# Two attention stages: one-bank units of maxima, a fourth score bank, three weighings in L1, the last folds on VectorE

## The reference

```python
# L0: 8 heads of 16; L1: 16 heads of 32 (with layer norms before its projections)
scores = einsum('bqhd,bkhd->bhqk', Qh, Kh) * scale
attn = softmax(scores, axis=-1)
ctx = einsum('bhqk,bkhd->bqhd', attn, Vh)
# then W_o, residual, and a feed-forward block
```

## Time and profile before

| | us |
|---|---|
| median of three runs | 6442.13 (6438.35 to 6446.0) |
| the profiled execution | 6450.87 |
| its span, first to last instruction | 6449.1 |
| PE busy / PE weight loads busy | 5748.3 / 3457.8 |
| DVE / ACT / POOL busy | 3664.2 / 3201.7 / 2617.4 |

### The profile page before, as it was taken

How to read it: one execution, slowest core, us unless ns; L and a number is a source line. 1 busy time by engine, 2 the same in 40 slices (tenths; PEclk the granted TensorE clock), 3 DMA queues, 4 the chain that set the end, 5 groups by cost and what they waited for, 6 DMA issues and landing times. The chain is left out here.

```text
span 6449.1 us, 99761 instructions
## 1 busy us (share of the span) xinstructions
PE 5748.3 (89%) x29508; PEld 3457.8 (54%) x29508; DVE 3664.2 (57%) x4012; ACT 3201.7 (50%) x5857; POOL 2617.4 (41%) x1284
## 2 busy tenths in 40 slices
PE   5869999999666569999999999999999997659999
PEld 4734444444255445555555555555555553447777
DVE  4457777777433556666666666666666663521111
ACT  3327776777422335555555555555555564022222
POOL 0000000000000028888888888888888886000000
PEclk9969999999878779999999999999999998779999
DMA  3431111111342321111111111111011102820000
GB/s 106 124 87 34 35 33 34 33 33 29 93 153 86 93 75 35 29 36 35 38 36 35 27 37 36 36 38 36 25 37 37 36 24 74 258 72 26 26 26 14
DMA packets 335740, 347.84 MB, mean 54 GB/s; under 512 B 183664, under 2 KB 187632, under 8 KB 333296
## 3 DMA queue, kind: packets, MB, share of 16 engines
q1 hardware_dynamic: 335344, 342.99, 19.9%
HBM read 227.57 MB, written 115.21 MB: 53 GB/s over the span
## 5 line engine op out<-in xcount | busy, mean ns | idle before, releaser
L750 DVE TENSOR_REDUCE a_maxes<-a_mscore 128x1 f32<-128x802 f32 (+1 forms) x3072 | 2931.6, 988 | 1360.5 <-PE a_mscore L787 1344.8
L732 ACT ACTIVATE a_prob<-a_score 128x512 f32<-128x512 f32 x4992 | 2600.4, 605 | 1524.2 <-PE a_score L797 1517.5
L797 PE MATMUL a_score<-a_q,a_k 97*128 97x512 f32 (+1 forms) x4992 | 1956.2, 446 | 64.4 <-ACT a_prob L732 39.7
L704 POOL TENSOR_TENSOR a_added<-a_added,a_prob 128x1024 f32<-128x1024 f32 x768 | 1829.1, 2382 | 230.9 <-ACT a_prob L732 181.9
L787 PE MATMUL a_mscore<-a_k,a_qm 96*128 96x512 f32 (+5 forms) x6144 | 1734.7, 400 | 85.2 <-DMA a_k<-k 55.7
L787 PEld LDWEIGHTS a_mscore<-a_k,a_qm 96*128 96x128 f32 (+1 forms) x6144 | 1483.5, 311 | 317.1 <-DVE a_maxes L750 226.0
L816 PE MATMUL a_acc<-a_prob,a_v 128*32 128x512 f32 x9984 | 1611.9, 608 | 0.0
L797 PEld LDWEIGHTS a_score<-a_q,a_k 97*128 97x128 f32 (+1 forms) x4992 | 885.7, 191 | 1311.6 <-ACT a_prob L732 800.3
L701 POOL TENSOR_TENSOR a_added<-a_prob 128x1024 f32<-128x1024 f32 x128 | 303.5, 2371 | 2562.7 <-ACT a_prob L732 2562.6
L811 PE MATMUL a_acc<-a_prob,a_ones 128*1 128x512 f32 x2048 | 966.2, 594 | 0.0
L1121 DVE TENSOR_TENSOR f_hl<-f_h,f_hh 128x512 fp32r<-128x512 f32 x160 | 110.7, 692 | 672.5 <-ACT f_hh L1100 672.5
(11 more groups left out here) (143 smaller groups left out, 3728.4 us busy)
## 6 DMA issues: line engine op xcount, KB each, us to landing
a_qm<-q SPq DMA_DIRECT2D x384, 64.0 KB, 1.8
a_q<-q SPq DMA_DIRECT2D x384, 64.0 KB, 1.8
acc<-a_acc_sb SPq DMA_DIRECT2D x384, 64.0 KB
o_part<-acc SPq DMA_DIRECT2D x24, 1024.0 KB, 11.0
a_k<-k SPq DMA_DIRECT2D x48, 416.0 KB, 5.8
mid<-o_xout SPq DMA_DIRECT2D x16, 1024.0 KB, 8.3
f_X<-mid SPq DMA_DIRECT2D x16, 1024.0 KB, 6.3
q<-pq_out SPq DMA_DIRECT2D x128, 128.0 KB, 2.1
```

The costliest lines, as they stand in the source:

```text
L704: pool.tensor_tensor(added[:], added[:], prob[:, 3 * i + 1:3 * i + 3], ALU.add).then_inc(add_done, 1)
L732: act.activation(prob[:, t], score[SCORES[it.j][t]][:], ACT.Exp, scale=SCALE).then_inc(exp_done, 1)
L750: dve.tensor_reduce(maxes[j][:, t, c:c + 1], mscore[u % 2][:, lo:hi], AX.X, ALU.max).then_inc(unit_read, 1)
L797: pe.matmul(score[SCORES[it.j][t]][:], kt[it.k][r:r + C, i * P:(i + 1) * P], qt[it.j][r:r + C, :], start=True, stop=True).then_inc(score_d ...
```

## The change

- Four score banks in place of three; they go round and round (`score_bank`), and a score waits for the exp of four tiles before.
- Three tiles of maxima of one bank in place of two of two. A unit is one matmul and one reduction: in L0 32 units an item (416 or 386 columns, the half of the array changes with each, opposite to that of the score tile beside it where there is one unit), in L1 28 (458 columns). A unit waits for the reduction that last used its bank, in most cases that of three units before.
- Each score tile has a unit beside it. In L0 tiles 3, 11 and 19 have three, in L1 tiles 3 and 18 have two. `early` is 16 in L0, 10 in L1.
- L1 is weighed in three batches of three slots, after tiles 9 (the item before's last), 15 and 25. `copy_at` moves from step 4 to 5.
- POOL makes seven additions an item (`ADDS`). The last three, of 512 columns each, go to DVE (`fold`), after its unit of tile 6 in the next item. POOL's first addition of an item waits for the first fold of the item before.

```diff
@@ -421,13 +421,12 @@
 GROUPS = ST // 2
-SCORES = [([0, 1, 2] * ST)[:ST], ([0, 2, 1] * ST)[:ST]]
-CHUNKS = 4
-UNITS = (NB // P) * CHUNKS
+BANKS = 4
 QB = T // NB
 class Layout:
@@ -448,39 +447,49 @@
             self.at = {0: (5, True), 2: (6, True), 4: (0, False), 6: (1, False), 8: (2, False), 10: (3, False),
                        12: (4, False)}
             self.copy_at = 3
-            self.units_at = (0, 2, 3, 5, 6, 8, 10, 11, 13, 15, 16, 18, 19, 21, 23, 24)
-            self.early = 8
+            self.CHUNKS, extra, self.early = 8, {3: 2, 11: 2, 19: 2}, 16
         else:
             self.ROWS, self.SIDE, self.SUMS = 128, 3, 1
             self.slots = [[(0, 3 * i), (1, 3 * i + 1), (2, 3 * i + 2), (3, ("one", 3 * i))] for i in range(8)]
             self.slots.append([(0, 24), (1, 25), (3, ("sum", None))])
-            self.batches = [[0, 1], [2, 3], [4, 5], [6, 7], [8]]
-            self.at = {1: (3, True), 3: (4, True), 5: (0, False), 8: (1, False), 11: (2, False)}
-            self.copy_at = 4
-            self.units_at = (0, 2, 3, 4, 6, 7, 8, 10, 11, 12, 15, 17, 18, 21, 23, 24)
-            self.early = 6
+            self.batches = [[0, 1, 2], [3, 4, 5], [6, 7, 8]]
+            self.at = {4: (2, True), 7: (0, False), 12: (1, False)}
+            self.copy_at = 5
+            self.CHUNKS, extra, self.early = 7, {3: 1, 18: 1}, 10
         self.HALVES = P // self.ROWS
         self.COLS = SPAD // self.HALVES
         self.NBATCH = len(self.batches)
+        self.UNITS = NB // P * self.CHUNKS
         tiles = [[t for i in b for _, t in self.slots[i] if not isinstance(t, tuple)] for b in self.batches]
         self.opens = {min(ts): b for b, ts in enumerate(tiles)}
         self.closes = [max(ts) for ts in tiles]
+        self.units_at, made = [], 0
+        for t in range(ST):
+            more = 1 + extra.get(t, 0)
+            self.units_at.append(range(made, made + more))
+            made += more
+        assert made == self.UNITS
+        bank = [i % 3 for i in range(2 * self.UNITS)]
+        if bank[-1] == 0:
+            bank[-1] = 1
+        self.bank = [bank[:self.UNITS], bank[self.UNITS:]]
+        around = bank + bank
+        self.back = [[next(d for d in range(1, 6) if around[at - d] == around[at])
+                      for at in range(i, i + self.UNITS)] for i in (2 * self.UNITS, self.UNITS)]
     def key_tile(self, t):
         return t % self.HALVES, t // self.HALVES
     def chunk(self, c):
-        if self.HALVES == 1:
-            wide = -(-S // (2 * CHUNKS)) * 2
-            lo, hi = c * wide, min((c + 1) * wide, S)
-            return [(0, at, min(NB, hi - at), at - lo) for at in range(lo, hi, NB)]
-        a = self.COLS // CHUNKS
-        rest = S - self.COLS
-        b = -(-rest // (2 * CHUNKS)) * 2
-        return [(0, c * a, a, NB - a), (1, c * b, min(b, rest - c * b), NB)]
+        half, at = (1 - c % 2, c // 2) if self.HALVES == 2 else (0, c)
+        keys = min(self.COLS, S - half * self.COLS)
+        wide = -(-keys // (2 * (self.CHUNKS // self.HALVES))) * 2
+        return half, at * wide, min(wide, keys - at * wide)
 class Item:
@@ -505,7 +514,8 @@
-ADDS = 10
+ADDS, FOLDS, FOLD_AT = 7, 3, 6
 def attention(nc, name, H, hd, q, k, v, row, acc_out, sums_out):
@@ -523,7 +533,7 @@
     APART = SUMS == 1
     PAIRS = H // 2
     LAST_KEYS = S - (ST - 1) * P
-    EARLY = L.early
+    UNITS, CHUNKS = L.UNITS, L.CHUNKS
     ACC_ROWS = P if not APART else 3 * 32 + 1
     with phase(nc, name) as (ctx, sb, ps, sem):
@@ -540,8 +550,8 @@
             ones = sb("ones", [P, 1], F32)
             added, total = sb("added", [P, 2, NB], F32), sb("total", [P, NB], F32)
-        score = [ps(f"score{i}", [P, NB]) for i in range(3)]
-        mscore = [ps(f"mscore{i}", [P, 2 * NB]) for i in range(2)]
+        score = [ps(f"score{i}", [P, NB]) for i in range(BANKS)]
+        mscore = [ps(f"mscore{i}", [P, NB]) for i in range(3)]
         acc = ps("acc", [P, NB])
         k_loaded = [sem(f"k_loaded{i}") for i in range(2)]
@@ -553,7 +563,7 @@
         filled = sem("filled")
         score_done, exp_done, pv_done = sem("score_done"), sem("exp_done"), sem("pv_done")
         unit_done, unit_read, neg_done = sem("unit_done"), sem("unit_read"), sem("neg_done")
-        add_done, acc_copied = sem("add_done"), sem("acc_copied")
+        add_done, fold_done, acc_copied = sem("add_done"), sem("fold_done"), sem("acc_copied")
         acc_stored = [sem(f"acc_stored{i}") for i in range(2)]
         LOADS = 16 * 3 * HALVES
@@ -577,24 +587,13 @@
                 yield from pair(p, False, False)
             yield from pair(PAIRS - 1, False, True)
-        def score_free(it, t):
-            b = SCORES[it.j][t]
-            same = [u for u in range(t) if SCORES[it.j][u] == b]
-            if same:
-                return it.n * ST + same[-1] + 1
-            if it.first:
-                return None
-            return it.n * ST + max(u for u in range(ST) if SCORES[1 - it.j][u] == b) + 1 - ST
-        def units_of(it, half_step):
-            if half_step not in L.units_at:
-                return None
-            u = L.units_at.index(half_step) + EARLY
-            if u < UNITS:
-                return None if it.last else (1, u)
-            return None if it.last_two else (2, u - UNITS)
+        def score_bank(it, t):
+            return (t + ST % BANKS * it.j) % BANKS
+        def units_of(it, t):
+            found = [divmod(u + L.early, UNITS) for u in L.units_at[t]]
+            return [(1 + more, u) for more, u in found if not (it.last or (it.last_two and more))]
@@ -692,27 +691,17 @@
             for it in items(pool) if APART else ():
-                base = it.n * ADDS
-                for i in range(1, 8):
+                for i in range(1, ADDS + 1):
                     pool.wait_ge(exp_done, it.n * ST + 3 * i + 3)
                     if i == 1:
                         if not it.first:
-                            pool.wait_ge(add_done, base)
+                            pool.wait_ge(fold_done, it.n * FOLDS - FOLDS + 1)
                         pool.tensor_tensor(added[:], prob[:, 1:3], prob[:, 4:6], ALU.add).then_inc(add_done, 1)
                     else:
-                        pool.wait_ge(add_done, base + i - 1)
+                        pool.wait_ge(add_done, it.n * ADDS + i - 1)
                         pool.tensor_tensor(added[:], added[:], prob[:, 3 * i + 1:3 * i + 3],
                                            ALU.add).then_inc(add_done, 1)
-                pool.wait_ge(exp_done, it.n * ST + ST)
-                pool.wait_ge(add_done, base + 7)
-                pool.tensor_tensor(added[:, 0], added[:, 0], prob[:, 24], ALU.add).then_inc(add_done, 1)
-                pool.tensor_tensor(added[0:LAST_KEYS, 1], added[0:LAST_KEYS, 1], prob[0:LAST_KEYS, 25],
-                                   ALU.add).then_inc(add_done, 1)
-                pool.wait_ge(add_done, base + 9)
-                if not it.first:
-                    pool.wait_ge(pv_done, it.n * NBATCH)
-                pool.tensor_tensor(total[:], added[:, 0], added[:, 1], ALU.add).then_inc(add_done, 1)
         @block.scalar
         def _(act):
@@ -728,8 +717,10 @@
                     b = L.opens[t]
                     act.wait_ge(pv_done, it.n * NBATCH - NBATCH + b + 1)
                     if APART:
-                        act.wait_ge(add_done, it.n * ADDS - ADDS + 2 * b + 1)
-                act.activation(prob[:, t], score[SCORES[it.j][t]][:], ACT.Exp, scale=SCALE).then_inc(exp_done, 1)
+                        act.wait_ge(add_done, it.n * ADDS - ADDS + min(L.batches[b][-1], ADDS))
+                        if b == NBATCH - 1:
+                            act.wait_ge(fold_done, it.n * FOLDS)
+                act.activation(prob[:, t], score[score_bank(it, t)][:], ACT.Exp, scale=SCALE).then_inc(exp_done, 1)
             for it in items(act):
                 for s in range(GROUPS):
@@ -744,15 +735,29 @@
         def _(dve):
             def maximum(n, j, use, u):
                 t, c = divmod(u, CHUNKS)
-                pieces = L.chunk(c)
-                lo, hi = pieces[0][3], pieces[-1][3] + pieces[-1][2]
+                _, _, wide = L.chunk(c)
                 dve.wait_ge(unit_done, n * UNITS + u + 1)
-                dve.tensor_reduce(maxes[j][:, t, c:c + 1], mscore[u % 2][:, lo:hi], AX.X, ALU.max).then_inc(unit_read, 1)
+                dve.tensor_reduce(maxes[j][:, t, c:c + 1], mscore[L.bank[j][u]][:, 0:wide], AX.X,
+                                  ALU.max).then_inc(unit_read, 1)
                 if u == UNITS - 1:
                     dve.wait_ge(unit_read, n * UNITS + UNITS)
                     if not (isinstance(n, int) and n < 2):
                         dve.wait_ge(row_stored[j], use * 16)
                     dve.tensor_reduce(negmax[j][:], maxes[j][:], AX.X, ALU.max, negate=True).then_inc(neg_done, 1)
+            def fold(n):
+                dve.wait_ge(add_done, n * ADDS + ADDS)
```

(67 more changed lines are left out.)

## The result

The changed kernel takes 7150.11 us (median of 4 runs, 7144.84 to 7160.17), the kernel before beside it 6440.24 (4 runs, 6438.31 to 6446.0): a ratio of 1.110, 95% interval 1.108 to 1.112. That is inside the range (6390 to 7170) and on the side that was given the most chance, but it is not the case that was forecast (6460). It is the rival "held twice by POOL" (7046, given 0.27), with clock falls on top. The profiled execution took 7160.17, span 7158.4.

The account below looks back on a forecast made before the run. No engine full; PE, issuing in order, waits for DVE's reductions. Profiled 6450.87 +112 (a0) -102 (a1) +6 (folds) +2 (starts) = 6469, less 9 to the runs' median: 6460 us; own range 6400 to 6550, 8 in 10 6390 to 7170.

Parts of the forecast that it names:

- Four score banks: Both attentions: the fourth bank buys nothing; in a0 the scores' wait for exps goes and a wait for DVE replaces it.
- held twice by POOL: Rival, a1: POOL's additions hold the second and third fold, third slot 4.6 us late, +586, 7046 us; chance 0.27.
- clock falls: PE's clock drops while it stands: up to 3.6 us an item, 461 in a1, up to 115 in a0's odd items.
- the forecast case: Whole kernel: the walks of both attentions plus the folds, 6460 us, own range 6400 to 6550, chance 0.43.
- a1's walk: Second attention: cycles of 8.46, 5.76 and 8.81 us, items of 23.03 for 23.83, -102 us.
- a0's walk: First attention: cycles of 3.69, 2.72 and 1.73 us, items of 21.35 on average with the seam, +112 us.
- the rival of cheap short reductions: Rival, both attentions: short reductions cost only their columns, a0 about +20, a1 180 more gain, 6188 us; chance 0.08.
- the seam: a0, tiles 11 and 13 of every other item: a unit waits for the reading two back, 0.78 us, 0.39 on average.
- The folds: a1, three additions on DVE, 0.69 us each, nothing for overlap with POOL's: 0.05 us late an item, +6 us.
- held once: Rival, a1: only the third fold waits for POOL, 2.24 us late, +287, 6747 us; once or in part, chance 0.22.

Follow-up runs that it names:

- a0 alone: First attention (a0) as in the changed kernel, second (a1) as in the kernel before: 6605.42 us, 1.024 of the kernel before.
- best of both: First attention as in the kernel before, second as changed but with POOL's first addition waiting for the third fold: 6333.05 us, 0.982 of the kernel before.
- the later release: Changed kernel with POOL's first addition of an item waiting for the third fold instead of the first: 6485.26 us, 1.006 of the kernel before.
- folds earlier: Changed kernel with the folds after the third score tile of the item instead of the seventh, release unchanged: 6989.84 us, 1.085 of the kernel before.

## Why the prediction was right and wrong

Right were the direction and the range, wrong the forecast case: 7150 for 6460, far outside its own 6400 to 6550. That the time lies in the wide range is owed to the rival that reached up to its end, 20 us above the measured time, and not to the forecast.

The three measured parts close the sum: a0's 160 (a0 alone), -112 for a1's walk (best of both) and +665 for the held folds (7150-6485) give +713; measured +710.

*a0's walk.* Right: cycles of 3.68 and 2.71, even items 20.9 for 20.96, odd ones without a clock fall 21.7 for 21.74. Reductions took 0.58 (416 columns) and 0.55 (386) for 0.59 and 0.56, so the rival of cheap short reductions fell. Wrong in size: +112 for a0 against 160. The missing 48 are the clock falls in odd items, which the forecast case held at nothing and the range at up to 115: the seam costs 101 with them and 25 without. In the trace of a0 alone the account nearly closes: its items lie 84 us in all above their lengths without a fall (20.90 and 21.69), those of the kernel before 23 above 19.55, and the last item, which has no units beside it, takes 16.4 us for 25.1; 84-23-9 = 52.

*a1's walk.* Right: items of 23.03 wherever the folds are not held, in four kernels (release after the third or second fold, folds on POOL, best of both). -102 was forecast for it, and the best of both measured -112, with the folds in it.

*The folds.* Here is the step that failed. "Below, its price is nothing" and "For the sum I go by the rows as they are, nothing" took a value for an overlap that no row showed, and made it the forecast, though the prediction's own rows (0.16 for POOL, 0.20 for DVE) said that the two meet in every item. The places were right: the first fold starts 5.09 after the cycle's score (5.08), POOL 5.86 (5.93). The rival's mechanism and its rule of decision were right too: POOL's start ahead of DVE's second fold. Both gaps were too long (0.08 and 0.139), but their order held.

*The size of the hold.* Worked out 4.58 an item, measured 27.1-23.03 = 4.07 in items without a clock fall. The walk gave each waiting instruction its full length after the other's end; the rows say otherwise: a held fold ends 0.54 after POOL's addition (4036.54+2.37 to 4036.59+2.86; full length 0.69), a held POOL addition 2.20 to 2.24 after the fold (2.38). Three such handovers make up the 0.5. For the same reason held once costs 24.84-23.03 = 1.81 where 2.24 was put down, and the experiment that moves one wait took 229 us more than the later release (6714-6485) for that rival's 287.

*Which items.* Counted over 126 items of a1 from the fold rows and the granted clock: 14 are held once (24.7 us; there the gap ahead of the second fold is 0.034, not 0.139), 19 held twice without a clock fall (27.1), 49 held twice with one spell at half clock (28.5), 44 with a double one (29.65). Times 128/126, the holds make 14x1.67+112x4.07 = 479, so 487 us; the clock falls 49x1.4+44x2.55 = 181, so 184 us; together 671 against the 665 measured. The forecast of up to 3.6 an item for the falls was a bound, and they came to 1.4 of it on average. The short gap comes in 16 of all 128 items, and in the same 16 with the release after the second or the third fold and with the folds earlier. They are just those whose folds run outside every loop of the program: in the first item of a head (the very first has none) or one of its last three, in the first and the last pair of heads, and behind the last item. In 14 of them POOL starts 0.144 after the fold that releases it, and 0.08 in the items of the loops. So both gaps go with the place in the code; what in a loop changes them is open.

*The clock.* In a1 the granted clock is 0.93 with the holds and 1.00 without them, in a0 0.90 with the seam and 0.98 without; idle matmuls (3.04 us) in one case and idle weight loads (1.00 and 0.54 close to each other) in the other stand at the fall to half speed (1.2 of 2.4 GHz). The Trainium skill, TensorE: Matmul & The Clock Gate, section HAM oscillation, says that waits between bursts of matmuls bring the clock down each time. The trace agrees in part: of 112 items held twice 93 show a fall and 19 none, and the waits at the seam are shorter than those of the section's example.

*Four score banks.* That they bought nothing is not shown by a run of its own. In 1000 us of a0 the loads' wait for exps went from 406 to 217 us and that for DVE's readings from 61 to 136. The waits for exps of 0.2 to 0.6 us, 300 before, are gone, as forecast; those left (246 of the 253 last 0.84) stand behind a weighing, with which PE is still busy.

## What to carry to other kernels

Before moving an addition from GpSimd to VectorE, look at what each of its instructions reads: here those with two inputs in SBUF and GpSimd's shut each other out for a whole instruction (2.86 us for 0.69), so release GpSimd only when the last of them is done, and put them where VectorE owes nothing to TensorE. Where a prediction finds that two instructions meet in every round and no row shows how they bear each other, the forecast belongs to the meeting, not to the row of each alone. And price a stall of TensorE with the clock that it costs: here short idle times of 1.00 and 0.54 us grew 25 us into 101, and the holds' 487 into 671.

## What the runs showed of the hardware

- A held instruction's bar begins when its semaphores are there and includes the time for which it is shut out: folds of 0.68 read 2.86 and 2.70, and DVE looks busier (1997 us in 2600) while it gets through a fifth fewer instructions than with the later release (2923 for 3601).
- Tens of nanoseconds decide hundreds of microseconds. DVE's next instruction starts 0.034 us after the one before it behind one wait of its own, 0.139 behind two in the 112 items in loops (0.034 in the other 16), POOL's 0.08 after DVE's (0.144 in 14 of the 16); which is first settles whether an item takes 27.1 or 24.84 us.
- The loser pays less than the winner's full length: the waiting fold ends 0.54 after the release for a length alone of 0.69 (0.68 on 2 partitions as well), POOL's 2.20 to 2.24 for 2.38.
- A reduction of the same 512 columns, with one input in SBUF and one column out, ran beside POOL at 0.686.
